# A mixture-of-experts kernel on one Trainium2 core: both experts of a token in one first product of the lower layer

## The reference

```
def kmoe(x_flat, W_router, A, B, scale, bias, ...):
    vals, idx = jax.lax.top_k(x_flat @ W_router.T, 2)
    probs = softmax(vals)
    Y = einsum('nkoi,nij,nkpj->nkop', A[idx], xs, B[idx])
    out = einsum('nkop,nk->nop', Y, probs)
    return out * scale + bias
h = gelu(kmoe(x, W_up, A_up, B_up, ...))      # 32 x 32 to 64 x 64
y = kmoe(h, W_down, A_down, B_down, ...)      # 64 x 64 to 32 x 32
```

## Time and profile before

| | us |
|---|---|
| median of 3 runs | 1376.27 |
| their range | 1375.77 to 1385.75 |
| the profiled execution | 1373.84 |
| its span, first to last instruction | 1372.0 |
| PE busy in the span | 1262.5 |
| VectorE busy | 799.0 |
| ScalarE busy | 444.6 |
| GpSimd busy | 227.8 |

### The profile page before, as it was taken

One profiled execution on the slowest core, in us unless ns is written; L12 is line 12 of the kernel. 1 busy time (PEld: TensorE's weight loads), 2 busy tenths in 40 slices (PEclk: granted clock), 3 DMA queues, 4 the chain that ended last, 5 costly groups with the idle time before them and its releaser, 6 DMA issues.

```text
span 1372.0 us, 61950 instructions
## 1 busy us (share of the span) xinstructions
PE 1262.5 (92%) x27944; PEld 817.2 (60%) x27944; DVE 799.0 (58%) x1495; ACT 444.6 (32%) x927; POOL 227.8 (17%) x372
## 2 busy tenths in 40 slices
PE   6999999999999999999999997977888888898886
PEld 4865333333333334676666675666777777787775
DVE  2264776776777671556556553637273845357766
ACT  0222131122122112222122221336363636246554
POOL 0000000000000001222122220225152433113212
PEclk9999999999999999999999998989999999669998
DMA  6677889989989973411100111003330306513102
GB/s 257 217 243 198 283 292 306 308 276 318 300 279 319 292 282 88 77 61 61 61 31 31 61 46 62 32 2 153 92 123 31 122 0 246 213 66 128 82 36 92
DMA packets 68080, 211.50 MB, mean 154 GB/s; under 512 B 14448, under 2 KB 30832, under 8 KB 53520
## 3 DMA queue, kind: packets, MB, share of 16 engines
q1 hardware_dynamic: 67984, 210.16, 45.5%
HBM read 172.37 MB, written 37.75 MB: 153 GB/s over the span
## 4 chain that ended last, share of the span: by engine, by line
PE 76%; DVE 9%; issue 5%; DMA 4%; POOL 2%; SPq 1%; ACT 1%; DVEq 0%; POOLq 0%; ACTq 0%
PE ps L686 14%; PE ps L537 10%; PE ps L1058 8%; PE ps L2104 5%; DVE arena L549 4%; PE ps L234 4%; PE ps L1172 4%; PE ps L1079 4%; PE ps L2058 4%; PE ps L2073 3%; PE ps L444 3%; PE ps L2090 2%; PE ps L676 2%; PE ps L2037 2%; PE ps L2147 2%
## 5 line engine op out<-in xcount | busy, mean ns | idle before, releaser
L549 DVE STREAM_TRANSPOSE arena<-arena 128x448 f32<-128x448 f32 (+1 forms) x512 | 263.4, 577 | 100.1 <-PE ps L537 81.9
L537 PE MATMUL ps<-arena 32*64 32x400 f32 (+1 forms) x4096 | 202.5, 506 | 0.8
L686 PE MATMUL ps<-arena 128*64 128x512 f32 x832 | 189.2, 598 | 0.0
L537 PEld LDWEIGHTS ps<-arena 32*64 32x64 f32 x4096 | 75.0, 130 | 97.5 <-issue 50.2
L686 PEld LDWEIGHTS ps<-arena 128*64 128x64 f32 x832 | 55.6, 136 | 121.3 <-issue 111.9
L570 ACT ACTIVATE arena<-ps,arena 128x384 f32<-128x384 f32 x64 | 36.3, 582 | 276.4 <-DVE arena L561 276.4
L1971 ACT COPY arena<-ps 128x512 f32<-128x512 f32 x128 | 75.1, 587 | 144.2 <-PE ps L2073 81.1
L1058 PE MATMUL ps<-arena 128*128 128x256 f32 x512 | 115.3, 383 | 0.8 <-ACT arena L993 0.8
L1058 PEld LDWEIGHTS ps<-arena 128*128 128x128 f32 x512 | 97.3, 192 | 17.5 <-issue 3.3
L1800 DVE SCALAR_TENSOR_TENSOR arena<-ps,arena 128x512 f32<-128x512 f32 x64 | 68.9, 1104 | 37.7 <-PE ps L2090 37.5
L2104 PE MATMUL ps<-arena 64*64 64x32 f32 x4096 | 84.7, 236 | 6.3 <-DVE arena L1817 5.7
(11 more groups left out here) (144 smaller groups left out, 1859.5 us busy)
## 6 DMA issues: line engine op xcount, KB each, us to landing
arena<-ctx SPq DMA_DIRECT2D x64, 1024.0 KB
arena<-ctx SPq DMA_DIRECT2D x32, 768.0 KB
arena<-q_n SPq DMA_DIRECT2D x64, 256.0 KB, 11.3
h_n<-arena SPq DMA_DIRECT2D x16, 1024.0 KB, 4.5
arena<-h_n SPq DMA_DIRECT2D x16, 1024.0 KB, 9.5
arena<-x SPq DMA_DIRECT2D x16, 512.0 KB, 4.4
arena<-ctx SPq DMA_DIRECT2D x32, 256.0 KB
x_n<-arena SPq DMA_DIRECT2D x16, 512.0 KB, 3.5
```

The source lines that it names most:

```text
L537: last = pe.matmul(ps[b * SEQ:(b + 1) * SEQ, tb, 0:WIDTH[tb]], qs[p % 2][r, db, b * SEQ:(b + 1) * SEQ], z[r, at % RING, b, 0:WIDTH[tb]], s ...
L549: vec.transpose(z[:, at % RING, :, g * 224:g * 224 + nt * 32].rearrange("p b (j t) -> p b j t", t=32), slots[slot_of(k)][:, :, 0:nt, db * ...
L686: last = pe.matmul(ps[b * SEQ:(b + 1) * SEQ, OB, :], probt[:, j, b * SEQ:(b + 1) * SEQ], slot[:, b, jj, :], start=j == 0, stop=j == TILES - 1)
```

## The change

In the lower layer `first_dn` makes one product for each token, with the columns of both experts side by side (64 columns), and puts even g on partitions 0 to 63 and odd g on 64 to 127. That is half as many matmuls, each twice as wide. `second_dn` is as it was and still wants expert k on the partitions of half k, so the copy out of PSUM regroups: four copies of 64 partitions x 256, one for each pair of e (the half that is read, even or odd g) and k (the half that is written). ScalarE does the two with e = 0 (`mid_out_dn`), VectorE the two with e = 1 (a new `mid_out`, in its queue before the staging and `y_out` of the same step). A new semaphore `s_md` counts VectorE's pairs; `first_dn` and `second_dn` wait for it beside ScalarE's `s_me`. The staging of h is split: VectorE does the first 32 of 64 values, GpSimd a new `stage_h` with the other 32, counted by `s_shp`, for which `first_dn` and SyncE's reload of h wait too.

```diff
@@ helpers
+    def regrouped(n, k):
+        u = n % 2
+        def of(e):
+            src = ps[e * F1:(e + 1) * F1, 2 * u:2 * u + 2, 0:256].rearrange("p t (g k x) -> p t g k x", g=4, k=2)
+            dst = mid[u][k * F1:(k + 1) * F1, :].rearrange("p (t g e x) -> p t g e x", t=2, g=4, e=2)
+            return dst[:, :, :, e, :], src[:, :, :, k, :]
+        return of
+
+    def staged_h(T, n, part):
+        q, at = in_piece(n)
+        return (st_h[n % 2].rearrange("p (g j) -> p j g", g=8)[:, part, :], h_of[T][:, q, part, at])
@@ SyncE, reload of h
                     sp.wait_ge(s_sth, STEPS * T + PIECE * (q + 1))
+                    sp.wait_ge(s_shp, STEPS * T + PIECE * (q + 1))
@@ GpSimd
+        def stage_h(T, n):
+            pool.wait_ge(s_h[T % 2], 64 * (T // 2 + 1))
+            pool.wait_ge(s_s1, UP + STEPS * T + n - 1)
+            pool.tensor_copy(*staged_h(T, n, slice(F1 // 2, F1))).then_inc(s_shp, 1)
...
         for T in range(T_N):
+            stage_h(T, 0)
+            stage_h(T, 1)
             for n in range(STEPS):
                 stage_b_dn(T, n)
+                if n + 2 < STEPS:
+                    stage_h(T, n + 2)
@@ VectorE
-            vec.tensor_copy(st_h[n % 2].rearrange("p (g j) -> p j g", g=8), h_of[T][:, q, :, at]).then_inc(s_sth, 1)
+            part = slice(0, F1 // 2)
+            vec.tensor_copy(*staged_h(T, n, part)).then_inc(s_sth, 1)
+
+        def mid_out(T, n):
+            vec.wait_ge(s_s1, UP + STEPS * T + n + 1)
+            vec.wait_ge(s_s2, UP + STEPS * T + n - 1)
+            for k in range(2):
+                last = vec.tensor_copy(*regrouped(n, k)(1))
+            last.then_inc(s_md, 1)
...
             for n in range(STEPS):
+                mid_out(T, n)
                 if n + 2 < STEPS:
                     stage_h(T, n + 2)
                 y_out(T, n)
@@ ScalarE
+        def mid_out_dn(n):
+            act.wait_ge(s_s1, n + 1)
+            act.wait_ge(s_s2, n - 1)
+            for k in range(2):
+                last = act.copy(*regrouped(n, k)(0))
+            last.then_inc(s_me, 1)
...
             for n in range(STEPS):
-                mid_out(UP + STEPS * T + n)
+                mid_out_dn(UP + STEPS * T + n)
@@ TensorE, first_dn
             pe.wait_ge(s_sth, n + 1)
+            pe.wait_ge(s_shp, n + 1)
             pe.wait_ge(s_me, n - 1 + UP + CREDIT)
+            pe.wait_ge(s_md, n - 1 + CREDIT)
...
-                    for k in range(2):
-                        last = pe.matmul(ps[k * F1:(k + 1) * F1, 2 * u + t, g * D1:(g + 1) * D1],
-                                         st_h[u][rows_t, g * F1:(g + 1) * F1],
-                                         two(st_a[u])[rows_t, k, g * D1:(g + 1) * D1], start=True, stop=True)
+                    half, at = g % 2, g // 2 * 2 * D1
+                    last = pe.matmul(ps[half * F1:(half + 1) * F1, 2 * u + t, at:at + 2 * D1],
+                                     st_h[u][rows_t, g * F1:(g + 1) * F1],
+                                     two(st_a[u])[rows_t, :, g * D1:(g + 1) * D1], start=True, stop=True)
@@ TensorE, second_dn
             pe.wait_ge(s_me, n + 1 + UP + CREDIT)
+            pe.wait_ge(s_md, n + 1 + CREDIT)
             pe.wait_ge(s_stb, n + 1 + UP)
```

More of the change, by code:

```diff
@@ L1270, in mixture_parts @@
     s_me = sem("mo_me")
+    s_md, s_shp = sem("mo_md"), sem("mo_shp")
     s_fold, s_xt, s_part, s_bias = sem("mo_fold"), sem("mo_xt"), sem("mo_part"), sem("mo_bias")
@@ L1496, in mixture_parts @@
     f.s_stx = s_stx
-    f.s_me = s_me
+    f.s_me, f.s_md, f.s_shp = s_me, s_md, s_shp
     f.s_fold = s_fold
@@ L1607, in mixture @@
     s_stx = first.s_stx
-    s_me = first.s_me
+    s_me, s_md, s_shp = first.s_me, first.s_md, first.s_shp
     s_fold = first.s_fold
@@ L1812, in stage_h @@
         def stage_h(T, n):
-            q, at = in_piece(n)
             if n == 0:
@@ L1841, in _ @@
         vec.sem_inc(s_ye, CREDIT)
+        vec.sem_inc(s_md, CREDIT)
         vec.sem_inc(s_ohe["dn"][1], CREDIT)
```

## The result

The changed kernel took 1407.36 us (median of 4 runs) against 1381.01 us for the kernel before in the same comparison. The quotient of these medians is 1.0191; the ratio on record is 1.0224, 95% interval 1.0178 to 1.0269. The four times of the kernel before lie in two pairs, at 1376 and at 1386 us, so either figure is good to about half a per cent. The forecast was 1397, with 1409 for rival B, the one in which TensorE's clock falls. Rival B is what happened, on top of the ring that the forecast rests on.

The account below looks back on a forecast made before the run. PE bounds the lower layer's steps at 1.73 us; the change makes a VectorE ring of 2.06 us the bound. +22.7 (T=1 to 3), +0.4 (T=0) and -1.8 give +21.3: 1395 profiled, 1397 us as median, range 1378 to 1411.

Parts of the forecast that it names:

- rival B: Lower layer, T=1 to 3: TensorE's clock falls, 0.19 us more in 45 turns, +12 in all, 1409 us; 27%.
- the ring: Lower-layer steps: `second_dn`, `y_out`, VectorE's two copies and the next `second_dn` form a closed loop of 2.06 us a turn.
- The bound that changes hands: Lower-layer steps: PE, the bound at 1.73 us a step, gives way to the ring through VectorE at 2.06.
- the register wait: Ring term from the copy's end to `second_dn`, with the wait ahead of the matmul: 0.33 us, lower bound 0.15.
- Rival A: Lower-layer steps: VectorE's copies overlap, the ring is 1.77 us, 1380 us or 1369 with the short lag; 20%.
- Rival C: Lower-layer steps: PE stays the bound at 1.29 us a step, some 26 us less, near 1350; 3%.
- 45 turns x 2.06: Steps of T=1 to 3: 92.7 us, plus 8.4 for `residual`, 101.1 against 78.4, so +22.7 us.
- T=0: Last token group's steps: 33.8 us of turns, 3.5 routing, 1.6 stall, 38.9 against 38.46, so +0.4 us.
- The gatherings: Ahead of the steps in each T: the gather's last piece comes 0.44 us earlier, -1.8 us in four groups.
- The routing: T=0: ten groups of small VectorE instructions lie in the ring, 3.8 us together, some 3.5 with overlaps.
- Covers: Lower-layer steps: ScalarE's copies (378 ns at most), GpSimd's copy (0.62 us) and VectorE's half staging stay hidden, costing nothing.
- The sum: Whole kernel: +22.7 for T=1 to 3, +0.4 for T=0, -1.8 ahead of the steps, total +21.3 us, giving 1397.

Follow-up runs that it names:

- e1: Changed kernel plus four matmuls with unread results behind each first product of the loop; 1398.31 us, ratio 1.0166.
- e2: Changed kernel with VectorE's two copies for step n+1 ahead of `y_out` of step n; 1365.82 us, ratio 0.9907.
- e3: Changed kernel with halves exchanged: VectorE regroups partitions 0 to 63, ScalarE 64 to 127; 1394.86 us, ratio 1.0119.
- e9: e6 with the two `residual` calls moved out of the steps into the next set's gathering; 1347.96 us, ratio 0.9763.
- e5: Changed kernel plus eight idle matmuls ahead of the first `second_dn` of T=1 to 3, none in the steps; 1406.72 us, ratio 1.0169.
- e6: Changed kernel with the edits of e2 and e3 together; 1357.32 us, ratio 0.9809.
- e7: Changed kernel with three of the four regrouping copies on ScalarE and one on VectorE, which waits for ScalarE's first; 1377.04 us, ratio 0.9959.
- e4: Changed kernel with all staging of h back on VectorE, none on GpSimd; 1407.52 us, ratio 1.0215.

## Why the prediction was wrong, step by step

**The bound that changes hands: right.** PE ceased to be what a step waits for; 59 of 64 second products wait for VectorE's copies.

**The ring: right in mechanism and size.** Forecast 2.06 us a turn at full clock, 2.05 in e1. The doubtful terms held: 0.33 from `y_out` to the copy (0.32), 0.46 + 0.42 for the pair (0.87), 0.33 for the register wait (0.33). e2 shows that it was a closed ring and not a load: with two calls exchanged it is gone. At half clock 2.25 was forecast, 2.23 came. Rival A falls by the rows of the turn, which show no overlap; e3 shows the overlap at the first of its boundaries. Rival C, PE as the bound at 1.29, was never near; e9 comes closest with 1.4.

**The step that failed: "45 turns x 2.06".** It took T=1 to 3 at 2.4 GHz. The rival with the falling clock was on paper with its price, 0.19 us a turn, but at 27% behind the likeliest case. Against a forecast of 101.1 us these sets took 109.0; with matmuls in the pauses (e1), 102.2. The 7.9 are 45 x 0.19 = 8.6 less the first turn or so of each set, which still ran at full clock. So in place of 2.06 us at a granted clock of 1.00 the runs show 2.23 to 2.25 at 0.50. The profile before held a warning that I weighed too lightly: in T=0 the steps do not bring the clock back by themselves, and the ring gives PE a wait in every turn. e5 shows that these waits are enough, without the pause ahead of a set. In e9, with shorter waits, the clock held through T=1 to 3, and in e3 it came back late in each set; why there and not elsewhere these runs don't settle.

**The gatherings: the sign was wrong.** -0.44 us in each set was forecast, -1.8 in all; the stretch from the gathering's first matmul to the first `second_dn` grew by 4.2. In T=2 and 3 the gathering, from its first to its last run of matmuls, now starts at half clock and takes 1.7 and 2.1 us longer, twice the 1 us that rival B put in, while T=1's, which began at half clock before as well, is unchanged at 16.8. So the term left out the clock. In e2 and e6, whose sets end at full clock, a gain is there: 18.24 and 18.32 us from the first gathering matmul of T=2 to its first `second_dn`, against 18.53 before and 20.34 after the change. In e7, where ScalarE has a copy more ahead of that product, it is 18.70.

**T=0:** 38.9 forecast, 36.90 measured. The stall of 3.12 us, of which I had kept half, is gone in all ten kernels with the change in them. Why it was there was not tried. The routing added 3.3 us to the turns against 3.5 forecast. `residual` made its step 1.43 us longer in four of six cases (3.66 against 2.23), forecast 1.4; the other two took 3.43 and 3.87.

**Covers.** ScalarE's copies took 365 ns, as bounded, and stayed hidden. GpSimd's half copy, put at 0.62 us, took 0.71 in the mean; hidden too while the ring was closed, as e4 shows.

**The sum.** From one profiled execution to the other, 1395.1 us were forecast (1373.84 + 21.3) and 1410.28 measured, 15.2 more. The 7.9 of the clock in the steps and the 6.0 by which the gatherings missed, less 2.0 for T=0, make 11.9; the 3.1 that had gathered ahead of the lower layer, which the change does not touch, bring it to 15.0. That the medians, 1397 and 1407.4, lie only 10 us apart is chance: the profiled execution of the changed kernel was 2.9 us above its median.

## What to carry to other kernels

Before a copy goes to another engine, write down what stands ahead of it in that engine's queue: an output copy that waits for the product which the new copy feeds closes a ring, and its length is the step, whatever TensorE saves. Such a ring is cheap to open, by making the next step's input ahead of this step's output; here that exchange alone took 42 us off the median, part of it by the clock, and it turned the change from a loss into a gain. A copy handed to a third engine has to fit into that engine's turn too: ScalarE took one over here and became the bound at 1.80 us. And where a change makes TensorE wait in each turn, price the turn at both clock levels, and the stretch behind it too.

## What the runs showed of the hardware

- Half the clock is not twice the time: 32 records of the 128x32 form take 0.46 us at a granted clock of 1.00 and 0.65 at 0.50, the 64x64 first product 0.69 and 1.13.
- GpSimd's copy of 128x256 elements with strides (L1763) took from 0.61 to 0.96 us in the changed kernel, 0.71 in the mean and 0.635 in the median; its copy of 128x512 (L1758) took 0.62. Half the elements are not half the time there.
- VectorE's staging of 128x256 and that copy of GpSimd's delay each other, and which one pays goes by which starts first. In the 24 pairs of the changed kernel with GpSimd's ahead, as at 1328.43 and 1328.48 above, GpSimd's takes 0.62 to 0.64 us and VectorE's mostly 0.79 to 0.86. In the 11 with VectorE's ahead (1330.71 and 1330.74), VectorE's takes 0.39 to 0.43, what it takes alone in most cases, and GpSimd's 0.80 to 0.88. What in the chip they contend for no run here shows.
- From the end of a regrouping copy to the second product behind a register wait it took 0.32 to 0.37 us wherever a turn was read (after, e1, e3, e7), as with ScalarE's copy before.
